# A pre-norm attention and mixture-of-experts layer on one core: weight pieces spread over the chunks' loads, and the expert results stored by lower and higher expert

## The chip, the cores and the metric

The kernel runs on one core of one Trainium2 chip. The metric is the device time of one execution in microseconds (us), as the median of several runs.

## What is computed

The input x has 2 sequences of 1024 tokens of width 128. First comes an attention layer on the normalised x, whose output is added to x; then a mixture of experts on the normalised sum, whose output is added again:

```python
def reference(x, ...):
    x = x + _L0_attn_ref(_layernorm(x), norm_w, Wq, Wk, Wv, Wqf, Wkf, Wout)
    x = x + _L0_ffn_ref(_layernorm(x), Wgate, bgate, W1, b1, W2, b2, Wg, bg, Wl, bl, W3, b3)
    return x
...
def _L0_attn_ref(x, ...):                      # 16 heads of 8
    h = rmsnorm(x, norm_w); q, k, v = h @ Wq, h @ Wk, h @ Wv
    lin = linear_attention_causal(taylor(q @ Wqf), taylor(k @ Wkf), v)
    win = sliding_window_attention(q, k, v)    # the last 64 tokens
    return x + concatenate([lin, win]) @ Wout
...
def _L0_ffn_ref(x, ...):                       # 8 experts, 2 for each token
    topv, topi = top_k(x @ Wgate + bgate, 2)
    combine = sum(one_hot(topi) * softmax(topv)[..., None], -2)
    z = (x @ W1[e] + b1[e]) * (x @ W2[e] + b2[e])
    o = silu(z @ Wg[e] + bg[e]) * (z @ Wl[e] + bl[e])
    return sum over e of combine[..., e] * (o @ W3[e] + b3[e])
```

The 2048 tokens are 16 chunks of 128. Each token goes to two of the eight experts, so the experts have 4096 rows between them.

## The kernel before

The program has one instruction stream for each of the five engines, written out by hand, with semaphores between them. Nothing is scheduled: an engine runs its instructions in the order of the code. Four stages follow one another.

**Projections** (to about 36 us): q, k and v, each split into three bf16 parts that are written to DRAM (`qa_parts`, `k_parts`).

**Attention** (about 36 to 227 us): 16 chunks `c` of four units `u`. For each chunk SyncE (SP) loads a stack of query and key parts back from DRAM (`load_stack`: 12 transfers, 768 KB, into `ks` and `qas`), one to two chunks ahead of its use, held back by three waits on TensorE (PE) of chunk c-2 and c-1. In unit u VectorE (DVE) first takes the row maxima of the next unit's scores (`mrow`, L1161) and then does the steps that belong to earlier chunks (`post`): the output projection's follow-up for chunk c-1, the router for c-2, and for c-3 the routing weights (`weights_row`, L1022 to L1034) and places (`places`, L1065 to L1075). PE may only write the next scores (L610) when the maxima of the unit before are taken. `vals[:, r, k]` holds, for each token of chunk r and each of its two experts, the routing weight and the number of the result row: `k * 2048 + token` for the better (k = 0) and the second-best expert (k = 1). Two scatters for each chunk, issued by GpSimd (POOL), write the normalised token with these two numbers into its expert's region of `routed` in DRAM.

The experts' weights lie in SBUF (`w12`, `wgl`, `w3`, `b3`, `biasT`), in room that the projections' parts take until chunk 4. SP loads them in 18 pieces (16 of them for four experts each), two after each chunk's stack, from chunk 6 to 14:

```python
first = NC - len(pieces) // 2 - 1
...
for dst, src in pieces[2 * (c - first):2 * (c - first) + 2] if c >= first else ():
    sp.dma_start(dst, src).then_inc(e_in, 16)
```

After the last chunk come two rounds of `post` without attention (`c` = 16 and 17), in which DVE, PE and POOL finish the router of the last chunks one after another (`places_and_row` for chunks 14 and 15); PE runs filler matmuls there (L491). Then DVE works out a table of the further tiles (L1194 to L1214).

**Experts** (about 245 to 377 us): NT = 39 tiles `j` of 128 routed rows. The first eight are fixed, tile j being expert j's first 128 rows; the 31 others (`MORE`) are read from the table, each with its expert and its row, and those that no expert needs are filled with padding rows whose result numbers are out of bounds. For a table tile SP also copies the expert's W1 and W2 to a buffer (`wb12`), and POOL its Wg and Wl (`wbgl`). The steps are pipelined over tiles: PE transposes tile j+2, multiplies W1 and W2 of tile j+1, W3 of j-1, Wg and Wl of j. At the end of a tile DVE weights the result (`yw`, L1248) and POOL scatters it to `results` (L1394) by the result numbers, padding rows being dropped; `y_out[k]` counts the scatters that have landed, by j % 4.

**End** (about 377 us to the end): SP and ScalarE (ACT) wait for all scatters; SP then loads the first half of `results` to `res[0]` (best experts), ACT the second to `res[1]`, in four groups of 256 KB each. DVE adds the two, adds the sum to `x_all`, and SP writes each group to `out`.

Of the kernel before, what the change touches and what calls it, by code (L numbers as in the profile page):

```python
# [6 lines left out]
ALU = mybir.AluOpType  # L7
# [9 lines left out]
CH = 128  # L17
NC = B * T // CH
# [22 lines left out]
NT = TOPK * N // CH + E - 1  # L41
MORE = NT - E
RESULTS = TOPK * N
EPS_LN, EPS_RMS, EPS_LIN = 1e-5, 1e-6, 1e-6
# [54 lines left out]
def build(nc, ins, con, out):  # L99
# [12 lines left out]
    with ExitStack() as ctx:  # L112
# [86 lines left out]
        egap = sb("egap", [CH, 1])  # L199
        wsum = sb("wsum", [CH, 1])  # L200
        parts2 = sb("parts2", [CH, 2, 2, E])
        place = sb("place", [CH, E])
# [62 lines left out]
            sem(n) for n in ("xaffine", "xh_ready", "x1_ready", "st2_done", "mv2_ready", "ve2_ready", "rstd2_ready", "h2_ready"))  # L265
        done = sem("done")
        settled = sem("settled")
# [12 lines left out]
             "silu_done", "o_ready", "y_ready", "b3w_ready", "y_weighted"))  # L280
        res_in = [sem(f"res_in{g}") for g in range(NG)]
        res_sum, out_sum = sem("res_sum"), sem("out_sum")

# [15 lines left out]
        def folded(c):  # L299

            return c % (T // CH) != T // CH - 1, c - c // (T // CH)

        def run_steps(engine, step, places=()):


            def expert_of(t):

                if t < E:
                    return t
                if t not in known:  # L310
                    if t == E:
                        engine.wait_ge(table_ready, 1)
                    known[t] = engine.value_load(table[0:1, 0, t - E:t - E + 1], min_val=0, max_val=E - 1)
# [12 lines left out]
        WRITES = 6  # L326
# [27 lines left out]
        def _(sp):  # L354
# [69 lines left out]

            halves = (slice(0, E // 2), slice(E // 2, E))
            pieces = [(w12[:, h, lo:lo + F], ins[n][h].rearrange("e d f -> d e f")) for lo, n in ((0, "W1"), (F, "W2")) for h in halves] + [
                (wgl[:, h, k, lo:lo + F], ins[n][h, k * 128:(k + 1) * 128, :].rearrange("e d f -> d e f"))
                for k in range(2) for lo, n in ((0, "Wg"), (F, "Wl")) for h in halves] + [
                (w3[:, h, k, :], ins["W3"][h, k * 128:(k + 1) * 128, :].rearrange("e d f -> d e f")) for k in range(2) for h in halves] + [
                (b3[:], split("b3")), (biasT[:], ins["biasT"].rearrange("p (e c) -> p e c", e=E))]  # L430
# [16 lines left out]
            def load_tile(j, k):  # L447

                if j >= 4:
                    sp.wait_ge(tx_ready, j - 3)  # L450
                    sp.wait_ge(meta_copied, j - 3)
                if j < E:
                    row = j * REGION
                else:
                    row = sp.value_load(table[0:1, 1, j - E:j - E + 1], min_val=0, max_val=E * REGION)
                sp.dma_start(xin[:, k, :], routed[bass.ds(row, CH), :]).then_inc(xin_ready[k], 16)
                if j >= E:
                    if j >= E + 4:
                        sp.wait_ge(x1w_ready, j - 3)
                    e = sp.value_load(table[0:1, 0, j - E:j - E + 1], min_val=0, max_val=E - 1)  # L460
                    sp.dma_start(wb12[:, k, :], w12[:, bass.ds(e, 1), :].rearrange("p a f -> p (a f)")).then_inc(wb12_in[k], 16)
# [5 lines left out]
            pad_regions(sp)  # L467
            for j in range(4, E):
# [3 lines left out]
            for j in range(E, NT):  # L472
# [12 lines left out]
        def _(pe):  # L485
# [245 lines left out]
            def step(j, k, turn, expert):  # L731
# [4 lines left out]
                if on(1):  # L736
                    q = (k + 1) % 2
                    w = w12[:, j + 1, :] if j + 1 < E else wb12[:, (k + 1) % 4, :]
                    if j + 1 >= E:
                        pe.wait_ge(wb12_in[(k + 1) % 4], 16 * ((j + 1 - E) // 4 + 1))  # L740
                    pe.wait_ge(xT_copied, j + 2)
# [21 lines left out]
                if on(0):  # L763
                    q = k % 2
                    w = wgl[:, j] if j < E else wbgl[:, q]
                    if j >= E:
                        pe.wait_ge(wbgl_ready, j - E + 1)
                    pe.wait_ge(z_ready, 2 * (j + 1))
# [156 lines left out]
        def _(dve):  # L925
# [92 lines left out]
            def weights_row(r):  # L1018

                n, b = r + 1, r % 2  # L1020
                dve.wait_ge(r_egap, n)
                v.tensor_scalar(wsum[:], egap[:], 1.0, None, ALU.add).then_inc(r_ws, 1)  # L1022
# [3 lines left out]
                v.tensor_tensor(vals[:, r, 1, 0:1], vals[:, r, 0, 0:1], egap[:], ALU.mult).then_inc(r_w2, 1)  # L1026
                dve.wait_ge(r_w2, n)
                v.tensor_tensor(parts2[:], onehot[:].rearrange("p k (a e) -> p k a e", a=1).to_broadcast([CH, 2, 2, E]),
                                vals[:, r].to_broadcast([CH, 2, 2, E]), ALU.mult).then_inc(r_tmp, 1)
# [6 lines left out]
            def places_and_row(r):  # L1036

                n, b = r + 1, r % 2
                dve.wait_ge(pos_ready, n)
                v.tensor_tensor(place[:], positions_of(r)[:, 0:E], count[:], ALU.add).then_inc(r_place, 1)  # L1040
# [13 lines left out]
                v.tensor_copy(slot[:, b, :], slotf[:]).then_inc(r_slot, 1)  # L1054
                dve.wait_ge(r_w2, n)
                v.tensor_tensor(parts2[:], onehot[:].rearrange("p k (a e) -> p k a e", a=1).to_broadcast([CH, 2, 2, E]),
                                vals[:, r].to_broadcast([CH, 2, 2, E]), ALU.mult).then_inc(r_tmp, 1)
# [204 lines left out]

            run_steps(dve, step, (2,))
            for g in range(NG):
                at = slice(g * GC, (g + 1) * GC)
                dve.wait_ge(res_in[g], 32)
                v.tensor_tensor(res[0][:, at], res[0][:, at], res[1][:, at], ALU.add).then_inc(res_sum, 1)
                dve.wait_ge(res_sum, g + 1)
                v.tensor_tensor(x_all[:, at], x_all[:, at], res[0][:, at], ALU.add).then_inc(out_sum, 1)

        @block.gpsimd
        def _(pool):
# [112 lines left out]
            def step(j, k, turn, expert):  # L1385
                if E <= j + 1 < NT:
                    if j + 1 >= E + 2:
# [39 lines left out]
```

## Time and profile before

| | us |
|---|---|
| median of 3 runs | 394.18 |
| lowest, highest run | 391.79, 398.92 |
| the profiled execution | 396.04 |
| its span, first to last instruction | 394.2 |

All times of rows are from the one profiled execution, counted from the start of its span; 1.84 us of that execution lie outside the span. TensorE's mean granted clock in it is 0.978 of full speed. A row's line number is that of the kernel before. The expert stage's tiles share SBUF room with the attention stage's, and go by its names in some rows: `qas` there is any of xT, x2, z, sg, o, yw and b3w, `kv_tok` is wb12 or wbgl, and `ks` at the end is `res`.

### The profile page before, as it was taken

To read this page: it belongs to the slowest core of one execution; us is meant where nothing else is said; L and a number is where in the kernel's file an instruction comes from. 1 tells how busy PE (TensorE), PEld (TensorE's weight loads), DVE (VectorE), ACT (ScalarE), POOL (GpSimd) and SP (SyncE) were. 2 spreads that over 40 slices of the span, in tenths; PEclk is the share of its full clock that TensorE was granted. 3 is DMA by queue.
4 is the path that set the end of the run, shared out by engine and by line. 5 is a ranking of instruction groups with operands and counts; after the bars stand their busy time and mean duration, and the time that the engine had idled before them with its cause. 6 is when DMAs were issued, how large, how long until landed. Compare 5 with 4: busy or idle time off the path is not lost.

```text
span 394.2 us, 15938 instructions
## 1 busy us (share of the span) xinstructions
PE 357.2 (91%) x5708; PEld 302.9 (77%) x5710; DVE 253.2 (64%) x1002; ACT 213.1 (54%) x574; POOL 219.2 (56%) x368
## 2 busy tenths in 40 slices
PE   6799899799999999999999988899999999999910
PEld 2457688688888787778888853899999999999910
DVE  4787565488886888868887765455555555555415
ACT  0577567356676665655665620655555555555400
POOL 5374644456875766667675454124666666666510
PEclk9999999899999999999999999999999999999975
DMA  7747989576769988849551002223343333333028
GB/s 200 204 134 136 175 159 157 149 98 91 190 152 164 165 183 185 192 80 153 125 138 46 19 32 61 64 84 122 126 133 118 124 124 120 121 123 116 13 60 261
DMA packets 89024, 50.23 MB, mean 127 GB/s; under 512 B 57002, under 2 KB 82252, under 8 KB 88946
## 3 DMA queue, kind: packets, MB, share of 16 engines
q1 hardware_dynamic: 85378, 43.43, 47.9%
q0 software_dynamic: 2272, 4.46, 3.5%
q10 hardware_dynamic: 1296, 1.31, 1.0%
q8 instruction: 47, 0.77, 0.9%
q14 instruction: 31, 0.25, 0.3%
HBM read 29.52 MB, written 11.98 MB: 105 GB/s over the span
## 4 chain that ended last, share of the span: by engine, by line
PE 81%; DVE 5%; DMA 5%; issue 3%; SPq 2%; POOL 2%; ACT 1%; ACTq 0%; POOLq 0%; DVEq 0%
PE ps L773 8%; PE ps L779 8%; PE ps L663 7%; PE ps L610 5%; PE ps L756 4%; PE ps L659 4%; PE ps L702 4%; PE ps L709 4%; PE ps L745 4%; PE ps L748 4%; PE ps L622 4%; PE ps L629 3%; PE ps L685 3%; DMA ks<-results 2%; PE ps L589 2%
## 5 line engine op out<-in xcount | busy, mean ns | idle before, releaser
L1360 POOL TENSOR_SCALAR_AFFINE_SELECT amat<-amat 128x512 f32<-128x512 f32 x64 | 41.0, 641 | 63.1 <-ACT amat L845 62.4
L1394 POOL DMA_INDIRECT results<-qas,mrowid x39 | 38.2, 980 | 66.2 <-DVE qas L1248 66.2
L858 ACT ACTIVATE pmat<-ps 128x512 f32<-128x512 f32 x64 | 38.4, 600 | 51.5 <-PE ps L663 51.5
L1161 DVE TENSOR_REDUCE mrow<-ps 128x4 f32<-128x512 f32 x64 | 43.8, 685 | 30.9 <-PE ps L610 30.9
L1230 DVE SCALAR_TENSOR_TENSOR qas<-ps,bcol,qas 128x128 f32<-128x128 f32 x78 | 26.8, 350 | 36.2 <-PE ps L779 32.4
L900 ACT ACTIVATE qas<-ps,bcol 128x128 f32<-128x128 f32 x78 | 24.4, 364 | 39.6 <-PE ps L745 39.6
L1240 DVE SCALAR_TENSOR_TENSOR qas<-ps,bcol,qas 128x128 f32<-128x128 f32 x78 | 23.9, 346 | 26.6 <-ACT qas L900 26.5
L845 ACT ACTIVATE amat<-ps 128x512 f32<-128x512 f32 x64 | 38.5, 601 | 1.9 <-DVE xscale L949 1.4
L1321 POOL DMA_INDIRECT routed<-routed_row,slot x32 | 32.6, 1018 | 10.3 <-issue 5.7
L663 PE MATMUL ps<-minus_ident,mlow 128*128 128x128 bf16 x256 | 35.5, 219 | 0.5 <-issue 0.5
L663 PE MATMUL ps<-minus_ident,mrow 128*128 128x128 bf16 x256 | 35.9, 220 | 0.0
L1304 POOL TENSOR_TENSOR phik<-u_tok 128x128 f32<-128x128 f32 (+3 forms) x112 | 33.8, 333 | 2.2 <-DVE u_tok L965 2.2
L773 PE MATMUL ps<-qas,kv_tok 128*128 128x128 f32 x248 | 32.8, 275 | 0.0
L779 PE MATMUL ps<-qas,kv_tok 128*128 128x128 f32 x248 | 32.8, 275 | 0.0
L1389 POOL COPY kv_tok<-wgl 128x1024 f32 x31 | 32.5, 1049 | 0.0
L779 PEld LDWEIGHTS ps<-qas,kv_tok 128*128 128x128 f32 x248 | 30.2, 192 | 0.0
L916 ACT ACTIVATE qas<-ps,bcol 128x128 f32<-128x128 f32 x78 | 28.6, 367 | 3.0 <-PE ps L773 2.2
L773 PEld LDWEIGHTS ps<-qas,kv_tok 128*128 128x128 f32 x248 | 30.1, 192 | 0.0
L709 PE MATMUL ps<-pmat,v 128*32 128x64 f32 x1024 | 26.9, 222 | 1.8 <-issue 1.6
L610 PE MATMUL ps<-ks,qas 114*64 114x128 bf16 x512 | 26.8, 226 | 1.8 <-DVE kv_tok L1003 0.7
L702 PE MATMUL ps<-amat,v 128*32 128x128 f32 x512 | 26.5, 279 | 0.2
L659 PE MATMUL ps<-qas,ks 114*128 114x64 bf16 x512 | 25.8, 194 | 0.0
(183 smaller groups left out, 930.7 us busy)
## 6 DMA issues: line engine op xcount, KB each, us to landing
kv_tok<-w SPq DMA_DIRECT2D x31, 256.0 KB
qa_parts<-wgl SPq DMA_DIRECT2D x12, 256.0 KB, 3.2
ks<-k_parts SPq DMA_DIRECT2D x32, 96.0 KB
qas<-qa_parts SPq DMA_DIRECT2D x32, 96.0 KB
xin<-routed SPq DMA_DIRECT2D x39, 72.0 KB, 1.9
ks<-k_parts SPq DMA_DIRECT2D x32, 64.0 KB
qas<-qa_parts SPq DMA_DIRECT2D x32, 64.0 KB
w<-in_W SPq DMA_DIRECT2D x4, 512.0 KB
```

The source lines that it names most:

```text
L610: t = mm(ps[r:r + WINDOW, SQ, (hh // 2) * CH:(hh // 2 + 1) * CH], qs[:, p, h, j * WINDOW:(j + 1) * WINDOW], ks[:, p, j, h, :], start=True, ...
L659: mm(ps[:, ST, hh * WINDOW:(hh + 1) * WINDOW], ks[:, p, j, h, :], qs[:, p, h, j * WINDOW:(j + 1) * WINDOW], start=(hh == 0), stop=False, s ...
L663: t = mm(ps[:, ST, pr * CH:(pr + 1) * CH], part[:, u % 2, pr:pr + 1].to_broadcast([128, 128]), minus_ident[:], start=False, stop=part is m ...
L702: mm(ps[32 * g:32 * g + 32, bank, 0:CH], slot32(v1[:, p, 1], 4 * u + g), amat[:, u % 2, g, :], start=False, stop=True, skip_group_check=True)
L709: t = mm(ps[32 * g:32 * g + 32, bank, at:at + WINDOW], slot32(v1[:, p, j], 8 * hf + hh), pmat[:, u % 2, hh, :], start=False, stop=True, sk ...
L773: t = mm(ps[:, G[h], 0:CH], w[:, r, half(h)], z[:, q, r, :], start=(r == 0), stop=(r == 1))
L779: t = mm(ps[:, L[h], 0:CH], w[:, r, F + h * 128:F + (h + 1) * 128], z[:, q, r, :], start=(r == 0), stop=(r == 1))
L845: a_(amat[:, u % 2].rearrange("p g t -> p (g t)"), ps[:, A, :], ACT.Square).then_inc(square_done, 1)
L858: a_(pmat[:, u % 2].rearrange("p g t -> p (g t)"), ps[:, ST, :], ACT.Exp).then_inc(exp_done, 1)
L1161: v.tensor_reduce(mrow[:, b], ps[:, SQ, :].rearrange("p (a k) -> p a k", k=CH), AX.X, ALU.max).then_inc(max_done, 1)
L1360: q.affine_select(out=amat[:, u % 2], in_=amat[:, u % 2], compare_op=ALU.is_ge, fill=0.0, base=0, pattern=[[0, 4], [1, CH]], channel_multi ...
L1394: q.indirect_dma_start(results, bass.IndirectOffsetOnAxis(mrowid[:, m:m + 1], 0), yw[:, m, :], None, bounds_check=RESULTS - 1, oob_is_err= ...
```

## The change

The 18 weight pieces become 34: those of four experts are cut into two experts each. From chunk 4 (`GC`) on, one piece at a time goes between a chunk's loads: one ahead of SP's wait for the linear scores, one between the two loads of queries, one after the stack.

The result rows are no longer numbered by better and second-best expert but by lower and higher expert number: in `weights_row` and `places_and_row` DVE compares a token's two expert numbers (`swap`) and exchanges the row numbers in `vals` where the better expert has the higher number. Three instructions are added for each chunk, and a wait. The fixed tiles are now the first seven (`DYN` = 7) and the very last, tile 38, which is the first 128 rows of expert 7; table tiles are 7 to 37, 31 of them as before. Expert 7 is never a token's lower expert, so the lower half of `results` is complete when tile 37 has landed. SP waits for 38 tiles and loads the lower half; DVE adds it straight to `x_all`; ACT waits for all 39 and loads the higher half, and DVE adds that.

```diff
+DYN = E - 1
...
+        def fixed(j):
+            return j < DYN or j == NT - 1
+        def fixed_expert(j):
+            return min(j, E - 1)
...
-        N_W, N_F, N_C, N_R, N_E = 3, 4, 3, 12, 18
+        N_W, N_F, N_C, N_R, N_E = 3, 4, 3, 12, 34
...
                 if c >= 2:
+                    load_piece(c)
                     sp.wait_ge(a_ready, n + 4)
                 load_queries(c, p, 1, lin_in[p])
                 if c >= 2:
+                    load_piece(c)
                     sp.wait_ge(st_ready, n + 4)
                 load_queries(c, p, 0, win_in[p])
                 load_keys(c, p, 1, keys1_in[p])
...
-            halves = (slice(0, E // 2), slice(E // 2, E))
+            pairs = [slice(e, e + 2) for e in range(0, E, 2)]
...
-            first = NC - len(pieces) // 2 - 1
+            def load_piece(c):
+                if c >= GC and pieces:
+                    dst, src = pieces.pop(0)
+                    sp.dma_start(dst, src).then_inc(e_in, 16)
             for c in range(2, NC):
...
-                for dst, src in pieces[2 * (c - first):2 * (c - first) + 2] if c >= first else ():
-                    sp.dma_start(dst, src).then_inc(e_in, 16)
+                load_piece(c)
...
-                if j < E:
-                    row = j * REGION
+                if fixed(j):
+                    row = fixed_expert(j) * REGION
                 else:
-                    row = sp.value_load(table[0:1, 1, j - E:j - E + 1], min_val=0, max_val=E * REGION)
+                    row = sp.value_load(table[0:1, 1, j - DYN:j - DYN + 1], min_val=0, max_val=E * REGION)
...
             for k in range(4):
-                sp.wait_ge(y_out[k], 16 * ((NT - k + 3) // 4))
+                sp.wait_ge(y_out[k], 16 * ((NT - 1 - k + 3) // 4))
             for g in range(NG):
-                sp.dma_start(res[0][:, g * GC:(g + 1) * GC], half_of_results(0)[:, g * GC:(g + 1) * GC]).then_inc(res_in[g], 16)
+                sp.dma_start(res[0][:, g * GC:(g + 1) * GC], half_of_results(0)[:, g * GC:(g + 1) * GC]).then_inc(low_in[g], 16)
...
             def weights_row(r):
+                v.tensor_tensor(swap[:], topf[:, 0:1], topf[:, 1:2], ALU.is_gt).then_inc(r_swap, 1)
+                dve.wait_ge(r_swap, n)
+                for k in range(2):
+                    t = v.scalar_tensor_tensor(out=vals[:, r, k, 1:2], in0=swap[:], scalar=float(N * (1 - 2 * k)), in1=vals[:, r, k, 1:2],
+                                               op0=ALU.mult, op1=ALU.add)
+                t.then_inc(r_ids, 1)
...
             run_steps(dve, step, (2,))
             for g in range(NG):
-                at = slice(g * GC, (g + 1) * GC)
-                dve.wait_ge(res_in[g], 32)
-                v.tensor_tensor(res[0][:, at], res[0][:, at], res[1][:, at], ALU.add).then_inc(res_sum, 1)
+                dve.wait_ge(low_in[g], 16)
+                v.tensor_tensor(x_all[:, group_at[g]], x_all[:, group_at[g]], res[0][:, group_at[g]], ALU.add).then_inc(res_sum, 1)
+            for g in range(NG):
+                dve.wait_ge(res_in[g], 16)
                 dve.wait_ge(res_sum, g + 1)
-                v.tensor_tensor(x_all[:, at], x_all[:, at], res[0][:, at], ALU.add).then_inc(out_sum, 1)
+                v.tensor_tensor(x_all[:, group_at[g]], x_all[:, group_at[g]], res[1][:, group_at[g]], ALU.add).then_inc(out_sum, 1)
```

`places_and_row` gets the same lines as `weights_row`, and the engines' steps ask `fixed(j)` where they asked `j < E`.

Three places show how instructions move. On SP, the stack of chunk 6 from the `valid` row on; before (`w` is w12):

```order
L405 DMA ks<-const_valid 1x2048
L389 DMA qas<-qa_parts 24x16x128
L389 DMA qas<-qa_parts 16x16x128
L389 DMA qas<-qa_parts 8x16x128
L389 DMA qas<-qa_parts 24x16x128
L389 DMA qas<-qa_parts 16x16x128
L389 DMA qas<-qa_parts 8x16x128
L395 DMA ks<-k_parts 24x16x128
L395 DMA ks<-k_parts 16x16x128
L395 DMA ks<-k_parts 8x16x128
L441 DMA w<-in_W 128x4x256 x2
```

and after, from the row behind `valid` to the last piece:

```order
L449 DMA w<-in_W 128x2x256
L400 DMA qas<-qa_parts 24x16x128
L400 DMA qas<-qa_parts 16x16x128
L400 DMA qas<-qa_parts 8x16x128
L449 DMA w<-in_W 128x2x256
L400 DMA qas<-qa_parts 24x16x128
L400 DMA qas<-qa_parts 16x16x128
L400 DMA qas<-qa_parts 8x16x128
L406 DMA ks<-k_parts 24x16x128
L406 DMA ks<-k_parts 16x16x128
L406 DMA ks<-k_parts 8x16x128
L449 DMA wgl<-in_Wg 128x2x256
```

Two pieces of 512 KB behind the stack became three of 256 KB, two of them ahead of query loads. On DVE, unit 0 and the start of unit 1 of an attention chunk; before:

```order
L1097 TENSOR_SCALAR h<-x_all,mv,rstd 128x128
L1022 TENSOR_SCALAR wsum<-egap 128x1
L1024 RECIPROCAL vals<-wsum 128x1
L1026 TENSOR_TENSOR vals<-vals,egap 128x1
L1028 TENSOR_TENSOR parts<-onehot,vals 128x32
L1034 TENSOR_TENSOR routed_row<-parts 128x16
L1161 TENSOR_REDUCE mrow<-ps 128x4
```

and after:

```order
L1131 TENSOR_SCALAR h<-x_all,mv,rstd 128x128
L1041 TENSOR_TENSOR swap<-topf 128x1
L1044 SCALAR_TENSOR_TENSOR vals<-swap,vals 128x1 x2
L1048 TENSOR_SCALAR wsum<-egap 128x1
L1050 RECIPROCAL vals<-wsum 128x1
L1052 TENSOR_TENSOR vals<-vals,egap 128x1
L1055 TENSOR_TENSOR parts<-onehot,vals 128x32
L1061 TENSOR_TENSOR routed_row<-parts 128x16
L1195 TENSOR_REDUCE mrow<-ps 128x4
```

Three instructions stand ahead of the routing weights, and so ahead of the next maxima. At the end of DVE's program, before:

```order
L1248 SCALAR_TENSOR_TENSOR qas<-ps,mweight,qas 128x128
L1267 TENSOR_TENSOR ks<-ks 128x512
L1269 TENSOR_TENSOR x_all<-x_all,ks 128x512
L1267 TENSOR_TENSOR ks<-ks 128x512
L1269 TENSOR_TENSOR x_all<-x_all,ks 128x512
L1267 TENSOR_TENSOR ks<-ks 128x512
L1269 TENSOR_TENSOR x_all<-x_all,ks 128x512
L1267 TENSOR_TENSOR ks<-ks 128x512
L1269 TENSOR_TENSOR x_all<-x_all,ks 128x512
```

and after:

```order
L1264 SCALAR_TENSOR_TENSOR qas<-ps,bcol,qas 128x128 x2
L1282 SCALAR_TENSOR_TENSOR qas<-ps,mweight,qas 128x128
L1264 SCALAR_TENSOR_TENSOR qas<-ps,bcol,qas 128x128 x2
L1282 SCALAR_TENSOR_TENSOR qas<-ps,mweight,qas 128x128
L1301 TENSOR_TENSOR x_all<-x_all,ks 128x512 x4
L1305 TENSOR_TENSOR x_all<-x_all,ks 128x512 x4
```

The eight additions are the same in number, but all four of the lower half stand ahead of all four of the higher half.

## Rows read from the trace of the kernel before

**Rows 1.** The page, its DMA queues: packets, MB, share of 16 engines.

```profile
q8 instruction: 47, 0.77, 0.9%
```

**Rows 2.** Stages: length, busy of PE, PEld, DVE, ACT, POOL, clock, DMA share, GB/s.

```profile
69.40:71.40 2.00, 0.04 (x1) 0.00 (x0) 0.57 (x2) 0.00 (x0) 0.59 (x2) 1.00 0.93 251
98.00:145.00 47.00, 46.76 (x1105) 38.23 (x1101) 38.01 (x151) 29.44 (x76) 32.09 (x69) 1.00 0.83 176
...
178.00:225.00 47.00, 46.97 (x1116) 38.74 (x1114) 37.99 (x155) 30.16 (x78) 29.93 (x62) 1.00 0.47 96
257.00:372.00 115.00, 115.00 (x1028) 114.86 (x1029) 62.12 (x283) 66.44 (x213) 66.93 (x67) 1.00 0.33 112
380.00:394.20 14.20, 0.00 (x0) 0.00 (x0) 5.51 (x8) 0.00 (x0) 0.00 (x0) 0.50 0.73 222
```

**Rows 3.** PE's timeline, its stops in attention: start, us, and in brackets idle before.

```profile
71.44 0.38 PE L590 MATMUL ps<-wout,catT 128*128 128x128 f32 x1 [2.00 <-issue]
...
156.55 0.22 PE L663 MATMUL ps<-minus_ident,mlow 128*128 128x128 bf16 x1 [0.50 <-issue]
...
168.44 0.31 PE L709 MATMUL ps<-pmat,v 128*32 128x64 f32 x5 [1.60 <-issue]
```

**Rows 4.** SP's timeline, two weight pieces behind a stack: start, us.

```profile
160.46 1.05 SPq L441 DMA_DIRECT2D wgl<-in_Wl  x2
```

**Rows 5.** SP's own waits ahead of the query loads.

```profile
SPq L389 <- PE ps L663: 11.0, 11, 2.3
SPq L389 <- PE ps L622: 9.5, 10, 1.3
```

**Rows 6.** DVE's timeline: start, us, and idle before in brackets.

```profile
133.01 0.68 DVE L1161 TENSOR_REDUCE mrow<-ps 128x4 f32<-128x512 f32 x1
...
174.61 0.14 DVE L1022 TENSOR_SCALAR wsum<-egap 128x1 f32<-128x1 f32 x1
174.78 0.16 DVE L1024 RECIPROCAL vals<-wsum 128x1 f32<-128x1 f32 x1
...
178.72 0.68 DVE L1161 TENSOR_REDUCE mrow<-ps 128x4 f32<-128x512 f32 x1
```

**Rows 7.** PE's timeline, the scores that follow these maxima.

```profile
134.07 0.30 PE L610 MATMUL ps<-ks,qas 114*64 114x128 bf16 x4
...
180.05 0.41 PE L610 MATMUL ps<-ks,qas 114*64 114x128 bf16 x8
```

**Rows 8.** DVE by line, 36 to 226 us: busy, mean ns, idle before.

```profile
L1026 DVE TENSOR_TENSOR vals<-vals,egap 128x1 f32<-128x1 f32 x13 | 4.2, 325 | 0.4
```

**Rows 9.** DVE's timeline, the last chunks' router.

```profile
231.87 0.17 DVE L1115 TENSOR_TENSOR logit<-ps,bgate 128x8 f32<-128x8 f32 x1
231.95 0.28 DVE L1118 TENSOR_TENSOR x_all<-ps,xh 128x128 f32<-128x128 f32 x1
...
237.70 0.17 DVE L1040 TENSOR_TENSOR place<-ps,count 128x8 f32<-128x8 f32 x1 [0.37 <-PE ps L550]
```

**Rows 10.** The chain that ended last, its last pieces: start, us, what.

```profile
378.07 2.11 DMA results<-qas,mrowid
...
381.71 8.30 DMA ks<-results
...
390.76 0.69 DVE x_all L1269
```

**Rows 11.** The timeline of the end, all engines.

```profile
374.98 0.96 POOL L1394 DMA_INDIRECT results<-qas,mrowid  x1 [2.11 <-DVE qas L1248]
...
380.34 1.83 SPq L478 DMA_DIRECT2D ks<-results  x4
385.19 0.69 DVE L1267 TENSOR_TENSOR ks<-ks 128x512 f32<-128x512 f32 x1 [7.89 <-DMA ks<-results]
```

**Rows 12.** The scatters of results: queue in 371.5 to 380.3 us; landing, all 39.

```profile
q0 software_dynamic: 96, 0.00, 0.8%
...
DMA to landing us min/median/max: 2.1/2.4/3.2
```

More of the change, by code:

```diff
@@ L200, in build @@
         wsum = sb("wsum", [CH, 1])
+        swap = sb("swap", [CH, 1])
         parts2 = sb("parts2", [CH, 2, 2, E])
@@ L281, in build @@
         res_in = [sem(f"res_in{g}") for g in range(NG)]
+        low_in = [sem(f"low_in{g}") for g in range(NG)]
         res_sum, out_sum = sem("res_sum"), sem("out_sum")
@@ L301, in folded @@
             return c % (T // CH) != T // CH - 1, c - c // (T // CH)
+        def fixed(j):
+            return j < DYN or j == NT - 1
+        def fixed_expert(j):
+            return min(j, E - 1)
         def run_steps(engine, step, places=()):
             def expert_of(t):
-                if t < E:
-                    return t
+                if fixed(t):
+                    return fixed_expert(t)
                 if t not in known:
-                    if t == E:
+                    if t == DYN:
                         engine.wait_ge(table_ready, 1)
-                    known[t] = engine.value_load(table[0:1, 0, t - E:t - E + 1], min_val=0, max_val=E - 1)
+                    known[t] = engine.value_load(table[0:1, 0, t - DYN:t - DYN + 1], min_val=0, max_val=E - 1)
                 return known[t]
@@ L439, in _ @@
                     write_parts(c)
-                for dst, src in pieces[2 * (c - first):2 * (c - first) + 2] if c >= first else ():
-                    sp.dma_start(dst, src).then_inc(e_in, 16)
+                load_piece(c)
+            assert not pieces
             sp.dma_start(routed[E * REGION:E * REGION + CH, :], padrows[:]).then_inc(padded, 16)
@@ L451, in load_tile @@
                     sp.wait_ge(meta_copied, j - 3)
[L452 to L453 removed]
+                if fixed(j):
+                    row = fixed_expert(j) * REGION
                 else:
[L455 removed]
+                    row = sp.value_load(table[0:1, 1, j - DYN:j - DYN + 1], min_val=0, max_val=E * REGION)
                 sp.dma_start(xin[:, k, :], routed[bass.ds(row, CH), :]).then_inc(xin_ready[k], 16)
[L457 to L458 removed]
+                if not fixed(j):
+                    if j >= DYN + 4:
                         sp.wait_ge(x1w_ready, j - 3)
[L460 removed]
+                    e = sp.value_load(table[0:1, 0, j - DYN:j - DYN + 1], min_val=0, max_val=E - 1)
                     sp.dma_start(wb12[:, k, :], w12[:, bass.ds(e, 1), :].rearrange("p a f -> p (a f)")).then_inc(wb12_in[k], 16)
@@ L467, in _ @@
             pad_regions(sp)
-            for j in range(4, E):
+            for j in range(4, DYN):
                 load_tile(j, j % 4)
@@ L471, in _ @@
             sp.wait_ge(padded, 16 * (E + 1))
-            for j in range(E, NT):
+            for j in range(DYN, NT):
                 load_tile(j, j % 4)
             for k in range(4):
-                sp.wait_ge(y_out[k], 16 * ((NT - k + 3) // 4))
+                sp.wait_ge(y_out[k], 16 * ((NT - 1 - k + 3) // 4))
             for g in range(NG):
-                sp.dma_start(res[0][:, g * GC:(g + 1) * GC], half_of_results(0)[:, g * GC:(g + 1) * GC]).then_inc(res_in[g], 16)
+                sp.dma_start(res[0][:, g * GC:(g + 1) * GC], half_of_results(0)[:, g * GC:(g + 1) * GC]).then_inc(low_in[g], 16)
             for g in range(NG):
@@ L737, in step @@
                     q = (k + 1) % 2
-                    w = w12[:, j + 1, :] if j + 1 < E else wb12[:, (k + 1) % 4, :]
-                    if j + 1 >= E:
-                        pe.wait_ge(wb12_in[(k + 1) % 4], 16 * ((j + 1 - E) // 4 + 1))
+                    w = w12[:, fixed_expert(j + 1), :] if fixed(j + 1) else wb12[:, (k + 1) % 4, :]
+                    if not fixed(j + 1):
+                        pe.wait_ge(wb12_in[(k + 1) % 4], 16 * ((j + 1 - DYN) // 4 + 1))
                     pe.wait_ge(xT_copied, j + 2)
@@ L764, in step @@
                     q = k % 2
-                    w = wgl[:, j] if j < E else wbgl[:, q]
-                    if j >= E:
-                        pe.wait_ge(wbgl_ready, j - E + 1)
+                    w = wgl[:, fixed_expert(j)] if fixed(j) else wbgl[:, q]
+                    if not fixed(j):
+                        pe.wait_ge(wbgl_ready, j - DYN + 1)
                     pe.wait_ge(z_ready, 2 * (j + 1))
@@ L1038, in places_and_row @@
                 n, b = r + 1, r % 2
+                v.tensor_tensor(swap[:], topf[:, 0:1], topf[:, 1:2], ALU.is_gt).then_inc(r_swap, 1)
+                dve.wait_ge(r_swap, n)
+                for k in range(2):
+                    t = v.scalar_tensor_tensor(out=vals[:, r, k, 1:2], in0=swap[:], scalar=float(N * (1 - 2 * k)), in1=vals[:, r, k, 1:2],
+                                               op0=ALU.mult, op1=ALU.add)
+                t.then_inc(r_ids, 1)
                 dve.wait_ge(pos_ready, n)
@@ L1385, in step @@
             def step(j, k, turn, expert):
-                if E <= j + 1 < NT:
-                    if j + 1 >= E + 2:
+                if 0 <= j + 1 < NT and not fixed(j + 1):
+                    if j + 1 >= DYN + 2:
                         pool.wait_ge(l_ready, 2 * j)
```

11 lines of the change are left out of this document (7 added, 4 removed).

## The prediction

> **What bounds the kernel now.** I read the stages first [rows 2]. In attention TensorE is busy for 46.76 of 47.00 us (98 to 145) and for 46.97 of 47.00 (178 to 225); in the expert stage for 115.00 of 115.00. No other engine is near that, so in these stretches only what stops TensorE, or what comes before it, costs time. The last stretch is of another kind: from 380.0 to 394.2 TensorE does nothing, the DMA share is 0.73 and DVE adds for 5.51 us. There the chain of waits counts [rows 10]: the last scatter of results takes 2.11 us from 378.07, the last 256 KB load of results lands 8.30 us after its issue at 381.71, so at 390.01, then come two additions, and after the second (390.76 + 0.69 = 391.45) another 2.75 us until the span ends, which is the last copy to `out`. That stretch is what the second half of the change shortens. The first half works on attention, where TensorE's waits hold no row for a stack that lands late, but three stops in which it waited for nothing that the profile shows ("issue" in [rows 3]): 2.00 us before 71.44, in chunk 2, 0.50 before 156.55 and 1.60 before 168.44, in chunks 9 and 10.
>
> **The end, which carries the sum.** Before, the eight loads of 256 KB are issued from 380.34 [rows 11], and the last lands at 390.01: 9.67 us. The first two have landed at 385.19, 4.85 us after the first issue [rows 11]; the other six need 4.82 us more, 0.80 each. After, the lower half waits for tile 37 alone. Its scatter is issued at 374.98 [rows 11], 3.09 us ahead of tile 38's, so the lower half's four loads start 3.09 us earlier, near 377.25. If the eight loads are one stream through the same DMA engines, all have landed 9.67 us later, at 386.9. DVE has added the lower half by then and does one addition (0.69, rows 11) in place of two: 387.6, and with 2.75 us for `out` 390.35. Against 394.2 that is **-3.9 us**.
>
> The bounds of it. The last three scatters move nothing in this run (96 packets, 0.00 MB, [rows 12]): tiles 36 to 38 hold padding only. After, tile 38 holds rows of expert 7, so its scatter moves bytes: 2.4 us to landing in the middle, 3.2 at most [rows 12], against 2.11. The higher half is then issued at 380.6 to 381.4. At best its first load takes no longer than the last copy to `out` alone, 2.75 us, and three follow at 0.80: 385.8, a gain of 5.0. At worst each keeps its time of before: 381.4 + 4.85 + 2.4 = 388.7, a gain of 2.1. I take the middle, since the sixteen DMA engines carry the same bytes in both.
>
> **DVE's added instructions.** Three for each chunk: the comparison, and two exchanges that wait for it. A dependent step starts 0.17 us after the one before it (174.61 to 174.78, [rows 6]), an independent one 0.08 (231.87 to 231.95, [rows 9]), so together 0.17 + 0.08 + 0.08, some 0.35 us. In attention they stand ahead of the next maxima. In chunk 11 the maxima ended at 178.72 + 0.68 = 179.40 [rows 6], and the scores that need them began at 180.05 [rows 7]: 0.65 us in hand. The tightest I found is chunk 8: 133.01 + 0.68 to 134.07, 0.38 us. So 0.35 us is hidden by TensorE's own queue: 0. If that cover is gone, TensorE pays the excess in each of 13 chunks (second rival). In the rounds after the last chunk there is no such cover. The weights of chunk 13 run right into the router's next step, which starts without an idle gap at 231.87 [rows 9]: +0.35. In chunk 15, DVE waits 0.37 us for TensorE behind the place where the three now stand [rows 9]; I price chunk 15, and chunk 14 like it, at the remainder, 0 to 0.1 each: **+0.5 us** in all, between 0.3 and 1.2.
>
> **The weight pieces.** 18 pieces become 34. SP issues two in 1.05 us [rows 4], so three instead of two cost it 0.5 us more for each chunk. Ahead of the two query loads SP waits 11.0 us in 11 waits and 9.5 in 10 [rows 5], about 1.0 us at each of the places where a piece now goes in, so the piece fills a wait and the loads keep their time. A chunk's weights fall from 1 MB to 0.75 MB and start two chunks earlier. No stack made TensorE wait before, so I price this at 0, unless the stops change; by the SP waits the cover lasts until a piece takes over 1.0 us to issue.
>
> Those stops are the open part. In the 2.00 us of the first one the DMA share is 0.93 [rows 2]; TensorE stopped in the middle of a group, as if its next instructions had not come, and they come by DMA too, in 47 packets of 16 KB [rows 1]. Shorter bursts of weights should make such a packet wait less. But the longest stop, from 69.4 on, lies in chunk 2, and the first weight piece comes behind chunk 6's stack: it fell under the loads of stacks and the writing of parts alone, and these stay. So of the 2.1 us (0.5 + 1.6) in chunks 9 and 10 I take a quarter, **-0.5 us**; the bounds are all of it, -2.1, and as much again in chunks 4 and 5, where pieces now run, +2.1. On this the Trainium skill speaks against the change: Runtime: NRT & Kernel Launch, section "Instruction fetch mechanics", says that fetching is hidden, as an engine dispatches more slowly than its instruction memory is filled. By that the pieces are worth nothing here and the sum is 0.5 us higher; the row of 1.6 us, in which no wait on a semaphore shows, does not agree with it.
>
> **The expert stage** keeps 39 tiles and 31 table tiles. Tile 7 now needs the table, and its loads stand behind SP's wait for it; it is loaded three tiles ahead. TensorE is busy for the whole of 115.00 us [rows 2], and nothing is added to it. POOL's and SP's work for tile 38 goes; neither is waited for. 0.
>
> **The sum.** -3.9 + 0.5 - 0.5 = -3.9 us. The profiled execution (396.04) would become 392.1. It is 1.86 us above the median of the runs shown, and the stops vary between runs, so I carry the difference over: 394.18 - 3.9 = **390.3 us**, 1.0% faster.
>
> **Rivals.** *The stops in attention go* with the shorter bursts: -3.9 + 0.5 - 2.1 = -5.5, 388.7, and with the best end (5.0) 387.6. For it speaks that both stops of chunks 9 and 10 fell while pieces of 512 KB were on their way; against it the stop of chunk 2.
>
> *DVE becomes the bound, and the kernel slower.* The multiplication at L1026, on one column, takes 325 ns in the mean [rows 8] where its neighbour takes 160 [rows 6]; something stretches small steps there. If each of the three is stretched like that, they cost 0.98 us. Then TensorE waits for the maxima 0.98 - 0.65 = 0.33 us in 13 chunks, 4.3, and 0.3 more in chunk 8; the rounds behind cost 0.98 + 2 x 0.61 = 2.2. With -3.9 at the end that is +2.9: 397.1. It turns to a loss from x = 0.82 on, where 13 (x - 0.65) + x + 2 (x - 0.37) = 3.9. Against it: L1022 and L1024, one column too, take 140 to 160 ns.
>
> *The end doesn't move.* The lower half's 1 MB is in the DMA queues when the last scatter's 64 KB come. If these land only behind all of it, at 377.25 + 4.85 + 3 x 0.80 = 384.5, the higher half is issued then, its last load lands 2.75 + 2.4 later, at 389.7, and the end is 393.1: a gain of 1.1 in place of 3.9, and 393.6 with +0.5 and 0 for the stops. Rows 12 speak against it: a scatter lands within 3.2 us even beside the expert stage's copies; but none of those is 1 MB.
>
> **How the numbers follow.** Chances: the forecast 0.58, stops gone 0.17, the end held up 0.15, DVE the bound 0.10. The range must leave out no more than 0.2: it goes from 387.0 (stops gone with the best end, 387.6, and a little scatter of runs) to 394.5 (the end held up, 393.6, with the upper bound of the rounds behind, +0.7), and leaves out the DVE rival and the ends. A measurement here can tell about 2% from no change: 7.9 us. Faster than 386.3 needs the second case and luck with the runs: 0.07. Slower than 402.1 needs more than the DVE rival: 0.04. Within 2%: 0.89.
>
> **What would show it.** In the profile after: the lower half's loads issued on SP some 3 us ahead of ACT's; DVE's four additions of the lower half before the last of the higher half lands, and the last addition to the end at about 2.75 us; scores (L610's successor) with no new wait on the maxima; fewer stops in which TensorE waits for nothing shown. The prediction is wrong if the last scatter takes over 4 us, if scores wait for maxima in most chunks, or if a stack lands late for want of DMA time.

## The result and the profile after

The changed kernel takes 402.77 us, median of four runs (399.69 to 404.69); the kernel before takes 394.33 beside it (391.79 to 398.92). The ratio is 1.0206, 95% interval 1.0148 to 1.0265: **slower, by 1.5 to 2.7%**, where 1.0% faster was forecast. Ratios, here and in the experiments, compare fast runs alone, so they are not the quotients of the medians given, which are of all runs. The profiled execution took 399.69 us (span 397.8), the shortest of the four; the profiled one of before 396.04 (span 394.2). So the traces show 3.6 us of span of a difference of 8.4 between medians.

Where the 3.6 us lie, by TensorE's timelines: from the first output projection to the last it is 3.8 us more (173.4 to 177.2 us), ahead of them 0.9 (57.65 to 58.59); from the last one to the first tile's transposition 0.8 more (14.48 to 15.26); the experts are equal (132.59 and 132.45 from there to the last scatter's issue); the end is 1.8 shorter (16.13 to 14.32).

TensorE's waits from 72 to 226 us in the profile of after (engine, line, what it waited for: us in total, times, longest):

```profile
PE ps L630 <- issue: 3.6, 2, 3.4
PE ps L609 <- DVE count L1101: 2.1, 6, 0.4
PE ps L729 <- issue: 0.3, 1, 0.3
```

Two rows are new. The second is a semaphore that the prediction did not look at: the matmul of the output projection (L609) waits for the counts of the router's places. The first holds a stop of 3.4 us. "Issue" means that the profile found nothing that ended the wait; below, the trace shows what did: it is a late stack.

**The wait for the counts.** The timeline of after around chunk 13's exchange, engines POOL, DVE and PE (start, us, engine, line, operation; idle time before in brackets):

```profile
200.55 0.65 DVE L1131 TENSOR_SCALAR h<-x_all,mv,rstd 128x128 f32<-128x128 f32 x1
201.06 0.65 POOL L1396 TENSOR_SCALAR_AFFINE_SELECT amat<-amat 128x512 f32<-128x512 f32 x1
201.13 0.85 DVE L1041 TENSOR_TENSOR swap<-topf 128x1 f32<-128x1 f32 x1
...
201.65 0.53 POOL L1353 COPY v<-kv_tok 128x128 f32<-128x128 f32 x2
...
202.01 0.26 DVE L1044 SCALAR_TENSOR_TENSOR vals<-swap,vals 128x1 f32<-128x1 f32 x2
202.19 0.14 DVE L1048 TENSOR_SCALAR wsum<-egap 128x1 f32<-128x1 f32 x1
...
203.08 0.68 DVE L1195 TENSOR_REDUCE mrow<-ps 128x4 f32<-128x512 f32 x1
...
204.28 0.17 DVE L1101 TENSOR_TENSOR count<-ps,count 128x8 f32<-128x8 f32 x1
...
204.59 0.46 PE L609 MATMUL ps<-wout,catT 128*128 128x128 f32 x2 [0.36 <-DVE count L1101]
```

The same place in the timeline of before:

```profile
174.03 0.66 DVE L1097 TENSOR_SCALAR h<-x_all,mv,rstd 128x128 f32<-128x128 f32 x1
...
176.49 0.17 DVE L1067 TENSOR_TENSOR count<-ps,count 128x8 f32<-128x8 f32 x1
...
177.47 0.49 PE L589 MATMUL ps<-wout,catT 128*128 128x128 f32 x2
```

From `h` to the end of `count` it was 2.63 us (176.66 - 174.03) and is 3.90 (204.45 - 200.55). Before, the counts were there 0.81 us ahead of the matmul (0.43 to 0.81 in the 13 chunks with a count); now they are 0.14 ahead of it, with TensorE idle: 1.27 - 0.81 + 0.14 = 0.60 us later. The insertion itself is 1.06 us (201.13 to 202.19), of which `swap`, one column, takes 0.85. It starts 0.07 us behind the start of POOL's select and ends 0.27 after the select's end, when POOL is half through two copies. Nine of the 14 such comparisons in chunks and rounds take 0.83 to 0.85 us, and each of these nine chunk periods is 11.72 to 11.96 us long, against 11.36 of an undisturbed chunk: 4.6 us together. In the two chunks where it takes 0.25 and no stop falls, the period is 11.14 and 11.15 (11.16 and 11.17 before). The Trainium skill has a rule for it (SBUF — State Buffer, "Who interferes with whom"): a VectorE instruction with two SBUF inputs contends with a GpSimd instruction that reads SBUF, and the order of issue decides which of them is blocked. For `swap` and for the one-input `wsum` (0.14) the rows agree; L1044, with two inputs beside the second copy, is not stretched, so the rule does not tell all of it.

**The stop in chunk 3.** PE's timeline and, in the second fence, SP's in the same stretch (L400 loads queries, L406 keys, L449 a weight piece; from 76.27 to 85.72 it is the stack of chunk 4):

```profile
84.49 0.43 PE L729 MATMUL ps<-pmat,v 128*32 128x64 f32 x16
88.30 0.41 PE L630 MATMUL ps<-ks,qas 114*64 114x128 bf16 x8 [3.37 <-issue]
88.64 0.66 PE L671 MATMUL ps<-ident,state_t 128*96 128x128 f32 x2
```

```profile
76.27 2.15 SPq L406 DMA_DIRECT2D ks<-k_parts  x3
...
78.94 0.43 SPq L449 DMA_DIRECT2D w<-in_W  x1
79.41 1.88 SPq L400 DMA_DIRECT2D qas<-qa_parts  x3
81.33 0.42 SPq L449 DMA_DIRECT2D w<-in_W  x1
81.79 1.40 SPq L400 DMA_DIRECT2D qas<-qa_parts  x3
83.23 2.49 SPq L406 DMA_DIRECT2D ks<-k_parts  x3
```

The matmul at 88.30 is the first of chunk 4's scores, and in the code TensorE waits ahead of it for that chunk's window queries (`win_in`, L622), which are the three transfers issued from 81.79 to 83.19. In the trace the last count of their semaphore comes at 88.20 us, 0.10 ahead of the matmul. So the stop is the wait for a late stack. Before, in SP's timeline and PE's:

```profile
75.09 2.15 SPq L395 DMA_DIRECT2D ks<-k_parts  x3
...
77.75 2.94 SPq L389 DMA_DIRECT2D qas<-qa_parts  x6
```

```profile
86.43 0.42 PE L610 MATMUL ps<-ks,qas 114*64 114x128 bf16 x8
```

There the same queries landed at 84.44, 1.99 us ahead of the scores; in after they come 3.28 behind TensorE, which is ready at 84.92. These 5.3 us have four parts. SP starts the stack 1.2 later (76.27 against 75.09), in both kernels right behind a wait of over 3 us for the parts' writes. From there to the end of the query loads' issue it takes 6.92 us (to 83.19) in place of 5.60 (to 80.69), since two pieces now stand between; before, SP did not wait for TensorE there (no such row from 74 to 82 us), so they had no wait to fill. The queries land 5.01 us behind that in place of 3.75. And TensorE is there 1.5 us sooner, since before had lost time in chunk 2 [rows 3].

The stretches around it (length, busy us of PE, PEld, DVE, ACT, POOL, clock, DMA share, GB/s):

```profile
84.00:88.30 4.30, 0.93 (x35) 0.64 (x34) 2.39 (x14) 1.15 (x3) 3.16 (x9) 1.00 0.93 128
88.30:92.00 3.70, 3.70 (x36) 2.74 (x40) 0.85 (x2) 1.38 (x4) 0.70 (x1) 0.55 1.03 187
```

After the stop TensorE is granted 0.55 for 3.7 us, close to the lower of its two levels (1.2 of 2.4 GHz), and like matmuls take 0.63 to 0.66 us in place of 0.38 to 0.43. That chunk's period is 16.26 us, 4.9 over 11.36: the stop and another 1.5. The data queue has half as much again to move, from 83 to 90 us, before and after (queue: packets, MB, share of 16 engines):

```profile
q1 hardware_dynamic: 2483, 0.61, 71.2%
```

```profile
q1 hardware_dynamic: 2763, 1.03, 94.9%
```

**The end.** The timeline of after, then its chain; they answer to [rows 10, 11]:

```profile
383.09 1.75 SPq L498 DMA_DIRECT2D ks<-results  x4
...
386.33 0.69 DVE L1301 TENSOR_TENSOR x_all<-x_all,ks 128x512 f32<-128x512 f32 x1 [3.62 <-DMA ks<-results]
...
388.19 1.79 ACTq L942 DMA_DIRECT2D ks<-results  x4
...
392.25 2.68 SPq L501 DMA_DIRECT2D out<-x_all  x4
```

```profile
383.48 4.55 DMA results<-qas,mrowid
...
389.53 4.29 DMA ks<-results
...
393.84 0.69 DVE x_all L1305
```

The lower half's loads leave before the last scatter, and it lands after 4.55 us (2.11 before), so the higher half starts at 388.19, 4.71 us behind the scatter's issue. The last addition is over at 394.53, and 3.27 us later the span ends (2.75 before), since the copies to `out` now come one behind the other at the end.

### The profile page after: what moved, and what is told of

Its sections match the earlier page's. It is cut to its first block, busy times and chain, and to the rows that moved or that the text cites. A ratio compares the mean times of both kernels' runs of the same rounds, so it can differ in the third digit from the quotient of the medians.

```text
span 397.8 us, 16022 instructions
## 1 busy us (share of the span) xinstructions
PE 359.3 (90%) x5708; PEld 303.3 (76%) x5710; DVE 260.8 (66%) x1050; ACT 213.1 (54%) x574; POOL 219.1 (55%) x368
## 4 chain that ended last, share of the span: by engine, by line
PE 72%; DVE 11%; issue 6%; DMA 4%; POOL 2%; SPq 2%; ACT 1%; ACTq 0%; POOLq 0%; DVEq 0%
PE ps L793 8%; PE ps L799 8%; PE ps L683 7%; PE ps L630 4%; PE ps L776 4%; PE ps L679 4%; PE ps L768 4%; PE ps L765 4%; PE ps L729 4%; PE ps L722 3%; PE ps L642 3%; PE ps L649 3%; PE ps L705 2%; PE ps L609 2%; PE ps L539 2%
## 5 line engine op out<-in xcount | busy, mean ns | idle before, releaser
L630 PEld LDWEIGHTS ps<-ks,qas 114*64 114x64 bf16 x512 | 16.3, 109 | 13.0 <-issue 5.0
```

Of the source, the lines that this page charges most:

```text
L630: t = mm(ps[r:r + WINDOW, SQ, (hh // 2) * CH:(hh // 2 + 1) * CH], qs[:, p, h, j * WINDOW:(j + 1) * WINDOW], ks[:, p, j, h, :], start=True, ...
```

## The experiments

Ratios are to runs of the kernel before on the same chip (medians of before 395.92, 396.94 and 396.50 in the three jobs). Where not said, a kernel computes everything.

**1. The change without its weight pieces**: the 18 old pieces, two behind each stack; exchange and results as in the change.

```
-                    load_piece(c)
+                for dst, src in pieces[2 * (c - first):2 * (c - first) + 2] if c >= first else ():
+                    sp.dma_start(dst, src).then_inc(e_in, 16)
```

> The change without its weight pieces: 18 pieces behind the stacks from chunk 6, as before; results by lower and higher expert, and the exchange on DVE, as in the change. Theory (the loss is the pieces' longer stops of TensorE, about 6 us of the 8.4, and the exchange, about 4, less 1.8 us won at the end): 396 to 397 us. Rival (the pieces are neutral, the stops only scatter, and the exchange on DVE is the whole loss): 402 to 403 us, as the change.

Measured: 400.13 us, ratio 1.0150 (1.0088 to 1.0213). TensorE waits for the counts 2.6 us in 7 waits, chunk periods are 11.92 to 11.96; the last scatter takes 4.63 us and the end 14.49. Both expected values missed: the loss without the pieces is larger than the theory's and smaller than the rival's. Most of it does not need the pieces.

**2. The pieces alone**: the kernel before with 34 pieces between a chunk's loads, from chunk 4.

```
                 if c >= 2:
+                    load_piece(c)
                     sp.wait_ge(a_ready, n + 4)
...
+                    load_piece(c)
                     sp.wait_ge(st_ready, n + 4)
```

> The kernel before with the 34 weight pieces between the loads from chunk 4 on, nothing else changed. Theory: 400 us, TensorE stops of 2 us and more in chunks 3 to 5 with no wait shown. Rival: 394 us, as before.

Measured: median 400.69 of six runs between 393.77 and 403.25; there is no ratio, and the lowest run is no slower than before. In the profiled execution (398.26) TensorE stops again for 2.7 us in chunk 3, until the queries of chunk 4 land (87.36, scores at 87.45), and the clock is low behind it:

```profile
87.40:92.00 4.60, 4.55 (x65) 3.12 (x65) 0.85 (x2) 2.34 (x7) 2.51 (x3) 0.63 0.91 193
```

**3. The exchange in another place**: the whole change, the three instructions moved from the start of the weights to unit 3 of the chunk before, behind the router's choice.

```
-                v.tensor_tensor(swap[:], topf[:, 0:1], topf[:, 1:2], ALU.is_gt).then_inc(r_swap, 1)
...
+                if u == 3 and has[2]:
+                    exchange(c - 2)
```

> The whole change, with DVE's three exchange instructions moved from the start of unit 0 (chunk r + 3) to unit 3 of chunk r + 2, where DVE was idle for 0.83 us before its next maxima. Theory: TensorE's six waits on the expert counts (2.1 us in the profile of the change) go, 2 to 4 us of 402.8: 399 to 401. Rival (the exchange is the whole loss): 393 to 395.

Measured: 400.40, ratio 1.0157 (1.0087 to 1.0228). No wait for the counts is left, and undisturbed periods are 11.36 again, but the stop in chunk 3 is there (queries landed at 88.22, scores at 88.31). TensorE's waits, 72 to 226 us:

```profile
PE ps L630 <- issue: 3.3, 1, 3.3
PE ps L599 <- issue: 1.3, 1, 1.3
PE ps L683 <- issue: 0.6, 1, 0.6
```

And DVE by line: in the new place the comparison takes 174 ns in the mean, while in after's place it takes 656 (first row: this kernel; second: after).

```profile
L1041 DVE TENSOR_TENSOR swap<-topf 128x1 f32<-128x1 f32 x14 | 2.4, 174 | 0.0
```

```profile
L1041 DVE TENSOR_TENSOR swap<-topf 128x1 f32<-128x1 f32 x13 | 8.5, 656 | 0.0
```

**4. The exchange alone**: the kernel before with the three instructions in the change's place, writing to a spare tile that nothing reads.

```
+                v.tensor_tensor(swap[:], topf[:, 0:1], topf[:, 1:2], ALU.is_gt).then_inc(r_swap, 1)
+                dve.wait_ge(r_swap, n)
+                for k in range(2):
+                    t = v.scalar_tensor_tensor(out=spare[:, k:k + 1], in0=swap[:], ...)
```

> The kernel before with the same three DVE instructions at the same place, writing to a tile that nothing reads; the wait for them stays out. Theory: the instructions alone cost 3 to 4 us, 397 to 398.5; the first of them is stretched to about 0.8 us where POOL issues a scatter. Rival: 402.

Measured: 402.58, ratio 1.0214 (1.0161 to 1.0267): these three instructions alone cost as much as the whole change, as the rival had it; my 397 to 398.5 was too low. The first of them is stretched, but beside POOL's select, not its scatter.

```profile
PE ps L591 <- DVE count L1081: 2.6, 7, 0.5
```

The rounds behind the last chunk take 0.77 us more, as in after.

**5. The results alone, exchange in unit 3**: the lower and higher halves, the old pieces.

```
-        N_W, N_F, N_C, N_R, N_E = 3, 4, 3, 12, 34
+        N_W, N_F, N_C, N_R, N_E = 3, 4, 3, 12, 18
...
+                if u == 3 and has[2]:
+                    exchange(c - 2)
```

> Results by lower and higher expert, the exchange in unit 3, and the 18 pieces as before: the change without its two supposed costs. Theory (the exchange in unit 0 costs some 6 us, the pieces some 5, the end wins 1.8): about 2 us faster than before, 394 beside 396. Rival (the exchange costs wherever it stands): 398 or more.

Measured: 394.57 (12 runs), ratio **0.9950** (0.9909 to 0.9991): faster than before, if barely clear of no change. That is what the end is worth without the rest, some 2.0 us (0.4 to 3.6); in the profile it is 14.40 us in place of 16.13. Its last scatter still takes 4.75 us:

```profile
378.10 4.75 DMA results<-qas,mrowid
```

**6. The pieces from chunk 6**: before, 34 pieces between the loads, but first at chunk 6, four a chunk until 9.

```
+                if c >= 6 and pieces:
...
+                for _ in range(2 if c < 10 else 1):
+                    load_piece(c)
```

> The kernel before with the 34 pieces between the loads, but from chunk 6 on, as the 18 were (four for each of chunks 6 to 9, then three). If the early start in chunk 4 is what costs: 395 to 397, as before, and no stop of 3 us near 85 us. If the place or size of the pieces costs: 400, as with the pieces from chunk 4.

Measured: ratio 1.0017 (0.9971 to 1.0062), no stop over 0.63 us. The places between the loads cost nothing that shows by themselves.

**7. The old pieces, from chunk 4.**

```
-            first = NC - len(pieces) // 2 - 1
+            first = GC
```

> The kernel before with its 18 pieces of 512 KB behind the stacks, two at a time, but from chunk 4 on (to 12). If the early start costs: 399 to 401 and a stop of 2 us or more near 85 us. If the place or size costs: 395 to 397.

Measured: ratio 1.0067 (1.0022 to 1.0113), a stop of 1.0 us in chunk 3 (the same queries, landed at 85.85, scores at 85.94): between the two expectations.

**8. Two of the four low loads held** until the last scatter has landed, in the kernel of experiment 5.

```
             for g in range(NG):
+                if g == 2:
+                    sp.wait_ge(y_out[(NT - 1) % 4], 16 * ((NT - 1) // 4 + 1))
```

> As the run with the exchange in unit 3 and the old pieces, but SP issues only two of the lower half's four loads ahead of the last scatter's landing, the other two behind it. Theory (the last scatter's 4.55 us come from the 1 MB of loads ahead of it in the DMA queues): the scatter takes 3 to 3.7 us, and the end is 0 to 1 us shorter. Rival (the scatter takes long because its rows are real): 4.5 us again.

Measured: ratio 0.9991 (0.9943 to 1.0039); the scatter takes 3.90 us, a little over what I expected, and the end 15.76 against 14.40, longer and not shorter.

**9. The pieces alone again**, the kernel of experiment 2 once more.

> The kernel before with 34 pieces of weights, one at a time between the loads of a chunk, from chunk 4 on; nothing else: the earlier run of this edit again, with more rounds. Theory (the early, interleaved pieces lengthen a stop of TensorE's instruction supply in chunk 3): slower by 0.8 to 1.6%, ratio 1.008 to 1.016, with a stop of 2 us or more between 84 and 90 us. Rival (the pieces cost nothing and the earlier run was chance): ratio within 0.995 to 1.005 and no stop over 1.1 us there.

Measured: six runs from 394.12 to 403.53, median 400.85, ratio 1.0142 (1.0093 to 1.0192). The ratio rests on the five runs from 398.63 up. The sixth, 394.12, is no slower than before, so the pieces cost time in most executions, not in each: over experiments 2 and 9 ten of 12 runs take 398 us or more, of before in the three jobs 23 of 69. The medians of all runs are 1.2 and 1.1% above those of before. The profiled run is the one at 394.12 and has no stop in chunk 3. It has one of 1.45 us in chunk 2, ahead of all pieces, and the low clock behind it, as before had after its 2.00 [rows 3]. With that TensorE comes to chunk 4's scores at 86.63, when the queries have been there for 0.57 us (86.06):

```profile
71.58 0.38 PE L598 MATMUL ps<-wout,catT 128*128 128x128 f32 x1 [1.45 <-issue]
```

```profile
72.00:78.00 6.00, 6.00 (x113) 4.99 (x114) 2.27 (x13) 2.56 (x7) 2.38 (x7) 0.72 0.47 131
```

**10. All four low loads held** until the last scatter has landed (as 8, with `g == 0`).

> The results part with the exchange moved, old pieces (the version that was 0.995 of before), but all four loads of the low half wait until the last scatter has landed, so that nothing of the 1 MB is in the queues beside the scatter. Theory (the scatter is held up by the low loads): the last scatter takes 2.1 to 2.9 us in place of 4.75, and the end from its issue to the end of the span is 15.0 to 16.1 us, no better than the 16.13 of before. Rival (a scatter with real rows is slow by itself): it still takes over 4 us.

Measured: ratio 1.0135 (1.0096 to 1.0174). The scatter is back to 2.24 us, so its delay is the low loads' 1 MB in the queues. The expected end was a miss: 19.07 us (376.93 to 396.0), not 15 to 16. The eight loads share the engines, DVE adds all low groups first, and the four copies to `out` begin only at 390.56.

```profile
376.93 2.24 DMA results<-qas,mrowid
380.57 8.64 DMA ks<-results
390.07 1.06 DVEq L113
391.13 1.20 DVE x_all L1299 x2
```

**11. The 34 pieces from chunk 4, three behind each stack**, none between the loads.

```
                 load_stack(c)
...
+                for _ in range(3):
+                    load_piece(c)
```

> The kernel before with 34 pieces from chunk 4 on, three in a row behind each chunk's stack, none between the loads. If the place between the loads is what costs: ratio 1.00 to 1.005, no stop over 1.1 us between 84 and 90. If the start at chunk 4 costs whatever the place: like the repeat of the pieces alone beside it, 1.008 to 1.016, with a stop of 2 us or more there. The old pieces from chunk 4 gave 1.0067 and a stop of 1.00.

Measured: ratio 0.9972 (0.9927 to 1.0017), a stop of 0.99 us in chunk 3. The window queries of chunk 4 land at 84.12, and the stop is a wait for its last keys (86.59, matmul at 86.68). Neither the number of pieces nor the start at chunk 4 costs by itself.

**12. The whole change without its two costs**: the exchange in unit 3, the pieces from chunk 6.

> The whole change with its two costs taken out: the exchange of ids in unit 3, and the 34 pieces between the loads from chunk 6 on. If the two costs are all that made the change slower, the end is left: ratio 0.992 to 0.999, no wait for the counts, no stop over 1.1 us in chunk 3. If something else in the change costs, the ratio is over 1.005.

Measured: 394.41 (12 runs), ratio 0.9979 (0.9949 to 1.0009); TensorE waits for no counts, its longest stop behind 72 us is

```profile
PE ps L631 <- issue: 0.7, 1, 0.7
```

and the end is 14.97 us, with a scatter of 5.30. It is not better than experiment 5; the two can't be told apart.

## Why the prediction was wrong

**The step that failed** is "So 0.35 us is hidden by TensorE's own queue: 0." It has two faults. First, it measured the slack at the wrong wait: between the maxima and the next scores (0.38 to 0.65 us). DVE's queue behind the insertion also holds `count`, and in unit 2 TensorE waits for it ahead of the output projection. The rows of matmul and count were in the trace, 0.43 to 0.81 us apart, and the wait (`r_count`) was in the code. Second, it priced the insertion at 0.35 us from undisturbed neighbours; in that place the first instruction takes 0.85 and the whole 1.06. The stretched row of [rows 8], which the prediction left to a rival, was a warning. Experiment 4 shows the cost alone (+2.1%), experiment 3 that the place makes it: the same three instructions in unit 3 leave no wait and periods of 11.36. The profile of experiment 4 accounts for 4.0 us in seven chunks (11.92 to 11.96) and 0.8 behind the last, 4.8 of the 8.5 that its ratio makes.

The rival "DVE becomes the bound" had the stretching and the sign, but the wrong wait, 0.325 us for each instruction where one takes 0.85, and the full gain at the end. So its 397.1 was still 5.7 us short.

**The rounds behind the last chunk**: +0.5 forecast, +0.78 measured, within the bounds. With the exchange in unit 3 (experiment 5) nothing is lost there (14.41 against 14.48).

**The end** was mis-sized: -3.9 forecast, -1.8 in the profile, some -2.0 in experiment 5, just outside the lower bound of 2.1. The scatter was taken at 2.4, at most 3.2, from a stretch without such loads; it took 4.3 to 5.3 in the five kernels that hold no load back, past the 4 us that the prediction named as a sign of being wrong. The rival that the end is held up had the mechanism (the low half's 1 MB ahead of the scatter), not its full size: the scatter lands during that stream, not behind all of it. Experiments 8 and 10 show it: 3.90 us with 0.5 MB in its way, 2.24 with none. Holding the loads loses more than the quicker scatter gives.

**The weight pieces**, priced at 0, cost 1.4% (0.9 to 1.9) in the runs that the ratio of experiment 9 takes. The step that failed is "so the piece fills a wait and the loads keep their time". The 1.0 us is a mean over 11 waits, and the stack that matters has none: SP comes late to chunk 4's stack, behind its wait for the parts' writes, and issues all six query loads of before in one go (77.75 to 80.69). TensorE had 1.99 us to spare there, against 4.5 and more for the stacks of chunks 5 to 13. The prediction's own sign, a stack that lands late for want of DMA time, came true: its queries land 3.3 us too late in after, and 1.5 us of low clock follow. The same wait is 2.7 and 3.3 us in experiments 2 and 3; in the fourth profile with early pieces between the loads (9) TensorE came late enough. In all 14 profiles every stop of 0.3 us or more from 84 to 89 us ends 0.09 or 0.10 us behind the last count of a load of chunk 4's stack; without early pieces between the loads none is over 1.3. So early and between the loads must come together: pieces from chunk 6 (6) leave this stack alone, and pieces behind it (11) come after its queries.

The bound named for the stops (2.1 us, in chunks 4 and 5) had the sign, but for another reason and too small. The stops of chunks 9 and 10, of which -0.5 was hoped for, are smaller in after (0.3), but they move about in all kernels.

**What stays open.** Why TensorE stops in chunks 2, 9 and 10: the three of before [rows 3] fall inside a run of matmuls with no wait between them, so they are not late loads. That they are late instructions, as the prediction supposed, no run shows. By the Trainium skill (Runtime: NRT & Kernel Launch, "Instruction fetch mechanics") fetching would be hidden; no run here separates it from another cause. The parts also do not add up: from experiment 5 on, early pieces (3) and the early exchange (1) add 2.1% and 2.0%, both together (after) 2.6%; with intervals of 0.4 to 0.7 each I draw nothing from it. And the timed runs of the slow kernels lie above their profiled ones (after: 401.78 to 404.69 against 399.69, at a granted clock of 0.971 to 0.976 against 0.980). One stretch at 0.55 for 3.7 us lowers the mean of 398 us by 0.004, so by estimate these runs had one or two more of them; where was not traced.

## What to carry to other kernels

Before an instruction is put in an engine's queue, list every semaphore that is raised behind it and measure the slack to each waiter; the tightest counts, not the one that comes to mind. Look at what the neighbouring engine runs at that moment, and move small work to a place where the two do not meet. Before a transfer is put ahead of another, look at the one place where the other has the least time to spare, not at the mean wait. A stop that a profile lays to nothing may still be a wait: look up in the code what is waited for there, and when it came. An early load that passes a last small write can hold that write up: count its bytes in the queues as part of the write's time.

## What the runs showed of the hardware

- A comparison of one column takes 0.14 to 0.25 us. Where it starts together with a 0.64 to 0.71 us select on GpSimd (0.01 us ahead of its start to 0.14 behind), it takes 0.71 to 0.85 (after, experiments 1 and 4).
- After a stop of TensorE of 1.45 us (experiment 9) or 3.37 (after), the granted clock is 0.72 in the mean of the next 6 us and 0.55 in the next 3.7; in after this adds 1.5 us to the stop's price. A stop of 1.82 us (experiment 1) left it at 1.00.
- A scatter of 0.07 MB lands in 2.24 us with nothing else in the queues and in 4.3 to 5.3 when 1 MB of loads is issued just ahead of it.
